# Layer 0: the second MLP product woven one matmul at a time between the transposes, and LN2's transposes of tiles 1 to 5 in PSUM bank 6

## What is computed

```python
h = _layernorm(x, n1_g, n1_b)                       # LN1
p = h @ w_in + b_in                                 # 96 -> 192
local = depthwise_3x3(p, k_conv)
mixed = 0.25 * (lr + rl + tb + bt) + local          # four exponential scans of local
mixed = _layernorm(mixed, on_g, on_b)
x = x + (mixed @ w_out + b_out)                     # "x2" below
h2 = _layernorm(x, n2_g, n2_b)                      # LN2
m = gelu(h2 @ w1 + b1) @ w2 + b2                    # 96 -> 384 -> 96
return x + m                                        # "x3" below
```

## Time and profile before

| what | value |
|---|---|
| time, median of 3 runs | 238.13 us (237.74 to 238.78) |
| span of the profiled execution, first to last instruction | 236.4 us |
| what lies between that span and the median | 1.7 us |
| PE busy with matmuls | 229.9 us, 97% of the span |
| weight loads | 186.2 us, 79% |
| DVE busy | 186.8 us, 79% |
| ACT, POOL busy | 133.3 and 127.7 us |
| granted TensorE clock | 1.000 of full speed, throughout |
| rounds 3 to 7 (the ones with `mlp2` before the last) | 41.4 to 104.7 us of the span |

### The profile page before, as it was taken

The page is one execution under the profiler, slowest core; times in us unless marked ns, Lnnn a source line. Parts: engine busy times, 40 slices in busy tenths (PEclk is TensorE's granted clock), DMA queues, the critical chain, the costliest instruction groups (busy, mean ns, idle before and its releaser), DMA issues.

```text
span 236.4 us, 4144 instructions
## 1 busy us (share of the span) xinstructions
PE 229.9 (97%) x1376; PEld 186.2 (79%) x1376; DVE 186.8 (79%) x470; ACT 133.3 (56%) x301; POOL 127.7 (54%) x161
## 2 busy tenths in 40 slices
PE   8999899999999999999999999999999999999995
PEld 6696767879696978787787877878787887878685
DVE  7699998999999999995467688695968778596741
ACT  5667886667675766465824927363472726353252
POOL 6464776897859492927685352415344341515120
PEclk9999999999999999999999999999999999999999
DMA  3851000000000000000000000010101001010102
GB/s 106 235 160 36 1 0 3 1 0 0 3 1 0 3 1 0 3 0 0 0 3 1 0 3 0 0 35 4 33 1 33 3 0 33 3 33 0 35 3 67
DMA packets 5637, 4.99 MB, mean 21 GB/s; under 512 B 528, under 2 KB 5360, under 8 KB 5616
## 3 DMA queue, kind: packets, MB, share of 16 engines
q1 hardware_dynamic: 5328, 4.64, 6.7%
q10 hardware_dynamic: 288, 0.09, 0.2%
HBM read 3.15 MB, written 1.57 MB: 20 GB/s over the span
## 4 chain that ended last, share of the span: by engine, by line
PE 40%; issue 28%; POOL 23%; DVE 6%; ACT 1%; POOLq 0%; DVEq 0%; ACTq 0%
POOL rs L367 8%; POOL hs L493 7%; PE pM L1213 7%; PE bank L1376 5%; POOL x4b L378 3%; PE bank L1411 3%; PE pM L1196 2%; PE bank L1184 2%; PE bank L1132 2%; POOL xl L364 2%; PE bank L1141 2%; PE bank L1416 2%; DVE cA L933 2%; PE pM L1198 2%; PE pM L1197 2%
## 5 line engine op out<-in xcount | busy, mean ns | idle before, releaser
L367 POOL TENSOR_TENSOR rs<-var,power 128x4 f32<-128x4 f32 x32 | 32.5, 1015 | 50.2 <-DVE var L832 46.7
L933 DVE SCALAR_TENSOR_TENSOR cA<-pA,cols,cA 128x528 f32<-128x528 f32 x54 | 40.9, 757 | 0.4
L1015 DVE SCALAR_TENSOR_TENSOR q<-th,bank 96x256 f32<-96x256 f32 x48 | 19.9, 416 | 10.9 <-PE bank L1257 10.5
L933 DVE SCALAR_TENSOR_TENSOR cB<-bank,cols,cB 128x256 f32<-128x256 f32 x56 | 26.6, 474 | 0.0
L1257 PE MATMUL pA<-q,a_half 96*96 96x256 f32 x96 | 24.8, 381 | 0.1
L1213 PE MATMUL pM<-w,hid 128*128 128x96 f32 x192 | 23.9, 272 | 0.0
L1213 PEld LDWEIGHTS pM<-w,hid 128*128 128x128 f32 x192 | 23.4, 192 | 0.5
L1510 PEld LDWEIGHTS pM<-w,hid 128*128 128x128 f32 x168 | 21.5, 192 | 1.1
L1376 PE MATMUL bank<-local,mix 128*128 128x384 f32 x64 | 22.1, 488 | 0.0
L364 POOL TENSOR_TENSOR xl<-xc,xh 96x512 fp32r<-96x512 f32 x15 | 19.0, 1270 | 5.6 <-ACT xh L537 4.8
L1510 PE MATMUL pM<-w,hid 128*128 128x96 f32 x168 | 21.5, 272 | 0.0
(11 more groups left out here) (245 smaller groups left out, 580.1 us busy)
## 6 DMA issues: line engine op xcount, KB each, us to landing
x_all<-in_x SPq DMA_DIRECT2D x8, 192.0 KB, 2.7
out<-y SPq DMA_DIRECT2D x7, 192.0 KB, 2.0
w<-in_w SPq DMA_DIRECT2D x1, 480.0 KB, 6.0
w<-in_w SPq DMA_DIRECT2D x1, 336.0 KB, 3.4
mix<-in_mix SPq DMA_DIRECT2D x1, 256.0 KB, 3.7
out<-y SPq DMA_DIRECT2D x2, 96.0 KB, 1.7
w<-in_w SPq DMA_DIRECT2D x1, 144.0 KB, 3.0
rows<-in_rows SPq DMA_DIRECT2D x1, 144.0 KB, 4.2
```

The lines of the kernel that those rows point to most:

```text
L367: pool.tensor_tensor(rs[:, :], var[:, :], power[:, :], ALU.pow).then_inc(step, 1)
L933: dve.scalar_tensor_tensor(out=acc, in0=src, scalar=col(f"k{'AB'[grp]}{k}"), in1=acc, op0=ALU.mult, op1=ALU.add).then_inc(s["conv_step"], 1)
L1015: dve.scalar_tensor_tensor(out=moved(c, k + 1)[0:D, half(h)], in0=th[c % 2][0:D, half(h)], scalar=1.0, in1=step_bank(k, h), op0=ALU.add, o ...
```

## The change

It does three things in `body0`. The 12 matmuls of `mlp2(e, 0..2)` are no longer issued in two blocks: one stands before and three between the first four transposes (cA), one behind each of LN1's four, and one behind each of LN2's four. LN2's transposes of tiles 1 to 5 write bank 6 instead of bank 0, and wait for the previous tile's third gelu (which reads bank 6) instead of `x1_split`. And w_out, which stays in bank 0, now waits in every round for the `x1_split` that the transposes waited for.

```diff
         def ln2_bank(t):
-            return bank[1 if t >= TILES - 2 else 0]
+            return bank[0 if t == 0 else 6 if t < TILES - 2 else 1]
...
-            def mlp2(e, j, psum):
+            def mlp2(e, j, psum, parts=range(CHUNKS)):
-                pe.wait_ge(s["gelu_done"], 3 * e + max(j + 1, 2))
-                for k in range(CHUNKS):
+                if 0 in parts:
+                    pe.wait_ge(s["gelu_done"], 3 * e + max(j + 1, 2))
+                for k in parts:
...
-                if j == HJ - 1:
+                if j == HJ - 1 and CHUNKS - 1 in parts:
                     last.then_inc(s["w2_done"], 1)
...
-                if g < TILES - 2:
-                    pe.wait_ge(s["x1_split"], 2 * min(g + 3, TILES - 1) + 2)
+                    if g == 0:
+                        pe.wait_ge(s["x1_split"], 8)
+                    elif g < TILES - 2:
+                        pe.wait_ge(s["gelu_done"], 3 * g)
...
-                if tile_known(e):
-                    mlp2(e, 0, bank[7])
+                def last_mlp(at):
+                    if tile_known(e):
+                        mlp2(e, at // CHUNKS, bank[7], [at % CHUNKS])
+
+                last_mlp(0)
...
                                 last = pe.transpose(bank[4 + k][:, part * P:(part + 1) * P],
                                                     acc[:, at + k * P:at + (k + 1) * P], ident[:, :])
+                                if grp == 0 and 2 * k + part // 2 < 3:
+                                    last_mlp(1 + 2 * k + part // 2)
...
-                        transposes(bank[0], xn1, s["trx_done"])
+                        for k in range(CHUNKS):
+                            transposes(bank[0], xn1, s["trx_done"], [k])
+                            last_mlp(CHUNKS + k)
...
-                if tile_known(e):
-                    mlp2(e, 1, bank[7])
-                    mlp2(e, 2, bank[7])
+                if not tile_known(f):
+                    for k in range(CHUNKS):
+                        last_mlp(CHUNKS + k)
...
-                if tile_known(g) and not mix_first(g):
-                    ln2_transposes(g)
+                for k in range(CHUNKS):
+                    if tile_known(g) and not mix_first(g):
+                        ln2_transposes(g, [k])
+                    last_mlp(2 * CHUNKS + k)
...
-                        pe.wait_ge(s["x1_split"], 6)
+                    pe.wait_ge(s["x1_split"], 2 * min(m + 2, TILES - 1) + 2)
```

More of the change, by code:

```diff
@@ L1180, in setup2, with transposes @@
                   .then_inc(s["l1_psum"], 1)
-            def transposes(dst, src, done):
-                for k in range(CHUNKS):
+            def transposes(dst, src, done, parts=range(CHUNKS)):
+                for k in parts:
                     last = pe.transpose(dst[0:D, k * P:(k + 1) * P], src[:, k * D:(k + 1) * D], ident[:, :])
-                last.then_inc(done, 1)
+                    if k == CHUNKS - 1:
+                        last.then_inc(done, 1)
             def last_three(dst, wh, wl, xh, xl):
@@ L1240, in gu, with ln2_transposes @@
                              xh3[0:D, :], xl3[0:D, :]).then_inc(s["gu_psum"], 1)
-            def ln2_transposes(g):
-                pe.wait_ge(s["xn2_ready"], 4 * g + 4)
-                pe.wait_ge(s["x2_ready"], 4 * g + 4)
-                if g < TILES - 2:
-                    pe.wait_ge(s["x1_split"], 2 * min(g + 3, TILES - 1) + 2)
-                elif g == TILES - 2:
-                    pe.wait_ge(s["conv_step"], conv_count(TILES - 1, 8, 1))
-                transposes(ln2_bank(g), xn2, s["tr2_done"])
+            def ln2_transposes(g, parts=range(CHUNKS)):
+                if 0 in parts:
+                    pe.wait_ge(s["xn2_ready"], 4 * g + 4)
+                    pe.wait_ge(s["x2_ready"], 4 * g + 4)
+                    if g == 0:
+                        pe.wait_ge(s["x1_split"], 8)
+                    elif g < TILES - 2:
+                        pe.wait_ge(s["gelu_done"], 3 * g)
+                    elif g == TILES - 2:
+                        pe.wait_ge(s["conv_step"], conv_count(TILES - 1, 8, 1))
+                transposes(ln2_bank(g), xn2, s["tr2_done"], parts)
             def rec_step(c, k):
@@ L1331, in body0 @@
                                                     acc[:, at + k * P:at + (k + 1) * P], ident[:, :])
+                                if grp == 0 and 2 * k + part // 2 < 3:
+                                    last_mlp(1 + 2 * k + part // 2)
                         last.then_inc(s["cT_done"], 1)
+                else:
+                    for at in range(1, CHUNKS):
+                        last_mlp(at)
                 if peeled(i, -1):
```

## The result

The changed kernel takes **240.82 us** (median of 6 runs, 240.13 to 241.26) against 237.91 for the kernel before in the same session. The ratio of the runs is 1.0105, with a 95% interval of 1.0084 to 1.0125: slower by one per cent, or 2.5 us (2.0 to 3.0). The two medians stand 2.9 apart. The forecast was 240.5, in a range of 237.0 to 241.3.

A forecast was written before the change was run, and what follows sets the result against it. PE sets the pace, DVE 0.5 us behind; after the change a loop over DVE bounds it. Round 3 +0.70, rounds 4 to 6 +1.2, round 7 reaching +2.4, round 8 -0.1: +2.3 on 238.1 gives 240.5 us, range 237.0 to 241.3.

The forecast's parts named there:

- PE is busy for practically all of its 13.0 us: Rounds 3 to 7 before the change: PE sets the pace, DVE half a microsecond behind it.
- They have 0.6 us of slack today: LN2's transposes on PE start 0.6 us after `xn2` ends; the second MLP product fills the time ahead.
- Which instruction a load stalls: PE's second MLP product: weight loads stall matmul instructions 0.027 us in a run, but not the one followed by a transpose.
- The residual L874 with 1 us and more of idle time: Sign in the new profile: DVE idles 1 us or more before its residual, which waits for the last matmul.
- The loop over DVE, 13.45: x2, `xn2`, LN2's first transpose, last matmul, residual, taps, next x2: 13.45 us a round against 13.04 now.
- Round 3, +0.70: Next x2 after round 3's `xn2`, last matmul, residual and taps comes at 53.41 against 52.71.
- Rounds 4 to 6, x2 at 91.84 is 1.9 late: DVE's loop adds 3 x (13.45 - 13.04) = +1.2 us, making that x2 1.9 late.
- Round 7, +2.4: Last LN2 transpose on PE at 99.72 against 97.28, delaying copies, `xl` and first MLP product by 2.4 us.
- Round 8, -0.1: No LN2 at that place and three stalls fewer on PE: 0.1 us saved.
- Sum +2.3: Whole kernel: the rounds' delays total +2.3 us, added to both the span of 236.4 and the median of 238.1.
- The gain of 1.5 if all is on the path: PE: 45 hidden stalls (1.2 us) plus `x1_split` waits (some 0.3); as a faster rival 236.6 us, 16%.
- only PE's loop counts: Rival: DVE has room for the late residual, PE's loop of 13.08 us decides; +0.9, 239.0 us; chance 14%.

The follow-up runs named there:

- experiment 12: e1 with e11's later `xb` sum on POOL (tiles 3 to 6), without waits by quarters; 237.69 us, 0.9967 of the kernel before.
- e3: Changed kernel with the first eight matmuls back in their old blocks, only LN2's transposes interleaved, bank 6 kept; 240.79 us, 1.0106 of the kernel before.
- e1: Changed kernel with the last four matmuls back in one block ahead of LN2's transposes; 237.40 us, 0.9962 of the kernel before.
- e9: Changed kernel with each LN2 transpose waiting only for its own quarter of `xn2`; 237.56 us, 0.9970 of the kernel before.
- e11: e9 with POOL's `xb` sum moved behind `xl` for tiles 3 to 6; 236.79 us, 0.9941 of the kernel before.
- e4: Changed kernel with DVE's residual L874 behind tap 5 instead of tap 3; 239.51 us, 1.0055 of the kernel before.
- e7: Kernel before with only the bank changes: LN2's transposes of tiles 1 to 5 in bank 6, matmul order as before; 238.05 us, ratio 0.9983.
- e2: e1 with LN2's transposes of tiles 1 to 5 in bank 0 again, waiting for `x1_split`; 238.61 us, 1.0019 of the kernel before.
- e5: Changed kernel with two of the last four matmuls ahead of LN2's first transpose, two behind; 238.16 us, 0.9990 of the kernel before.
- e6: Changed kernel with one of the last four matmuls ahead of LN2's first transpose, three behind; 239.46 us, 1.0040 of the kernel before.

## Why the prediction was right, step by step

- **"PE is busy for practically all of its 13.0 us".** By its records. But about 0.13 us of each of rounds 4 to 7 were a wait for `xl` under the mixing product's record (experiment 12 shows how that is read), so POOL already had a hand in the pace.
- **"They have 0.6 us of slack today", and PE stands still for 0.6.** Measured 0.75, 0.45, 0.68, 0.60 and 0.97 of idle time in rounds 3 to 7; counted as the forecast counts, from PE's arrival, it is 0.84 in round 5. The arrival was to be 2.66 after the round's start and was (68.56 to 71.22).
- **Which instruction a load stalls.** The size, 0.027 us, and the sum for a pair were right, the place was not. The short steps (0.085 us) are those behind the first matmul instruction after another kind of instruction, not those of the last one before a transpose: in the kernel before, the two records of 248 ns in round 5 are the first of each block (67.69 and 69.64). So the change frees 10 and not 9 steps a round; the mixing product's first step takes the tenth back, 0.352 in place of 0.325.
- **The residual L874 with 1 us and more of idle time.** 1.08, 0.82, 0.89, 1.44 and 0.71 in rounds 3 to 7: mostly below.
- **The loop over DVE, 13.45.** Measured 13.39 to 13.43 in rounds 4 to 6. In round 5 by its terms: x2 to `xn2`'s end 5.03 (5.02 forecast); semaphore 0.05 (0.10: the row of `xl` had shown 0.05, I rounded up); first transpose to the residual 1.53 (1.14 + 0.38); residual to x2 6.82 (6.81). Sum 13.43.
- **Round 3, +0.70.** The period is 13.72 against 13.04 (x2 at 39.67 and 52.71 before): +0.68.
- **Rounds 4 to 6, x2 at 91.84 is 1.9 late.** It starts at 93.82, 1.98 late, of which 0.2 was there at x2 of round 2 already (39.87 against 39.67).
- **Round 7, +2.4.** The last LN2 transpose starts at 99.80, against 97.28 before: +2.5, with the same 0.2.
- **Round 8, -0.1.** The span grew by 2.58, and round 8 starts 2.64 later (104.73 to 107.37): -0.06.
- **Sum +2.3.** By span +2.6, by the ratio +2.5, by the medians +2.9. Of the span's, 0.2 lie ahead of round 3, and from x2 of round 2 to the end it is +2.4. These 0.2 tell nothing of the change: x2 of round 1, ahead of all matmuls that were moved, starts anywhere from 26.48 to 27.44 in the 14 traces, and e3, which is as slow as the change, has its x2 of round 2 at 39.44, sooner than the kernel before. That 240.5 lies within 0.3 of the median is in part luck: it was added to a median of 238.1, and the one of the session was 237.9.
- **The gain of 1.5 if all is on the path.** PE's busy time fell by 0.9, but records cover waits as well, so that isn't the saving. As a time it was never seen whole: e1, which hides 8 of the 11 loads of a full round and keeps the bank, gains 0.8 against the kernel before beside it. POOL's queue and LN2's late transposes each hold a round at 12.75 or so (e9, e12); to get to -1.3 (e11) both had to go.
- **Rival "only PE's loop counts", 239.0.** e4 is this case made real, and gave 239.5, 1.3 over the kernel before where the rival has 0.9. The step that was off is its sum of 13.08: the branch over the mixing product is longer, 13.15, and I hadn't added it up. With it the rounds give 0.43 + 3 x 0.11 + 0.56 = 1.3.
- **Rival "the order hides no load".** It falls. A transpose with a matmul behind it takes 0.305 us (70.00 to 70.61 for two), where in blocks it was 0.110 + 0.222 = 0.332 by the earlier trace rows: one stall of 0.027 less. By the rule weighed there (the Trainium skill, *TensorE: Matmul & The Clock Gate*, "LDWEIGHTS" and "Back-to-back issue gap") both would be the same; the trace doesn't agree for these float32 transposes. What fails is the stream's part. The second of these sections gives columns over 2.4 plus 2.5 ns for matmuls without their loads, which is 56 ns for 128 columns, and about 81 ns in a stream of loads and matmuls; LN1's transposes stand 0.109 apart.
- **"The bank itself costs nothing."** Right (e7), but with the interleaving it is worth far more than the 0.3 that I gave it: 1.2 us (e2 against e1).

Shown by runs: that the loss comes from the four matmuls behind LN2's wait alone (e1, e3), that it grows with their number (e5, e6), that DVE's residual carries 1.3 us of it (e4), and that it goes when the wait is cut into quarters (e9). Round 4 is longer than round 5 in most versions, the fastest too (12.95 against 12.63 in e11). In e11 two things make it up. x2 of round 3 starts as soon as w_out is there (0.16 of idle time ahead of it), that of round 4 follows DVE's taps and starts 0.20 later behind w_out; and on PE, the third part of the first MLP product starts 0.20 us after w_out's last instruction in round 3 and 0.03 after it in rounds 4 to 7, in the kernel before as well. PE's rounds 4, 5 and 6 themselves take 12.63, 12.59 and 12.59 from start to start. What stays open is what holds that third part in round 3, and why e9's rounds 5 and 6 differ (12.70 and 12.82).

## What to carry to other kernels

PE did its matmuls in the order of the code: four that needed nothing more stood behind a transpose that waited (0.68 us in round 5). So an instruction that hides a stall of 27 ns shouldn't be put behind one that waits for another engine: ask of each moved instruction who waits for it, and whether the thing that it now stands behind is there in time. If an interleaving is wanted across a wait, first cut the wait to what each piece needs; here that turned +2.5 us into -0.7, by the ratios. And sum every branch behind the moved instruction, not only the one that you think of: two of the bounds here lay at 12.76 and 12.75 us a round, so an edit that took away one of them showed nothing until the other was gone as well.

## What the runs showed of the hardware

In round 5 the first transpose behind a wait holds up its follower a little: its record is 0.31 us long in place of 0.27, and the matmul behind it starts after 0.15 in place of 0.11. From the end of POOL's `xn2` to PE's start were 0.05 us (72.01 to 72.06). Of the 24 matmul instructions of a round, the fastest takes 248 ns and the slowest 275 or 276 in both kernels, and over the whole run the mean fell from 272 to 265: the stall is there or it isn't, and what stands ahead of the instruction decides. The steps between float32 matmul instructions in rounds 5 of the two kernels are 0.085 us for 96 columns where nothing stalls, 0.109 for the transposes' 128 with 96 or 128 columns to load, and 0.322 for the mixing product's 384: 0.84 to 0.89 ns a column.
